# A two-layer graph network on one core: the products of the neighbour sums cut from 256 to 128 columns, each half with its own load of the counts

## The chip, the core and the metric

The kernel runs on one core of a Trainium2 chip. The core has five engines that run their own instruction streams and meet through semaphores: TensorE (PE, matrix products; its loads of the stationary operand are shown as PEld), VectorE (DVE), ScalarE (ACT), GpSimd (POOL) and SyncE (SP), and 16 DMA engines that they share. The metric is the device time of one execution in microseconds, lower is better.

## The reference, cut to what matters

A graph has 3125 nodes with 128 features and 100000 edges sorted by their target node. Two blocks are applied one after the other: a mean-aggregating network of two layers, then a network of two layers that aggregates in four ways. What matters here is what is summed or compared over each node's edges:

```python
# first block, twice
summed = segment_sum(x[src], dst)
mean   = summed / max(deg, 1)
out    = x @ W_self + mean @ W_neigh + b
# second block, twice (layers l = 0, 1)
h       = xi[dst] + xj[src] + b_pre
mean    = segment_sum(h, dst) / degc
mean_sq = segment_sum(h * h, dst) / degc
std     = sqrt(relu(mean_sq - mean * mean) + eps)
mx, mn  = segment_max(h, dst), segment_min(h, dst)
out = concat(x, agg, agg * amp, agg * att) @ W_post + b_post   # agg = mean, mx, mn, std
out = out @ W_lin + b_lin
```

A layer norm and a residual follow each layer.

## The kernel before

The nodes lie in 25 blocks (`NT`) of 125 (`NB`). In a first stage the kernel counts, for each pair of a target block and a source block, how many edges go from each source node to each target node; these counts are exact in bf16 and are stored to DRAM (`counts`, 25 blocks of 800 KB). A sum over the edges is then a matrix product: for a target block b, the sum over the 25 source blocks a of counts(a, b) transposed times the features of a. The features are split into three bf16 parts (`XS[.., a, c, ..]`, c = 0 to 2) whose sum is the fp32 value, so one target block takes 25 x 3 = 75 products. `add_block` (L1186 to L1195) issues them into one bank of PSUM, with the counts `A[.., slot, a, :]` as the stationary operand, loaded for each product, and 128 or 256 columns of `XS` as the moving one:

- first sums (inside the stage that makes the counts) and second sums (`second_sums`, L1520) have width 128 (`F`), 75 products for each of 25 blocks each;
- each of the two main scans (`main_scan`, one for each layer of the second block) has width 256: the values and their squares side by side, 75 products for each of 25 blocks.

**The main scan** also finds the maximum and minimum over the edges, in two ways. For each target node, up to one edge from each of 20 source blocks (`PICKED`) is picked by a product with a matrix of ones and zeros (`select`, L1295, product L1308; 6 products of 500 columns for two source blocks and four target blocks); the other edges, at most 432 in each of 128 lanes (`REST`), are gathered row by row and scanned. The work is laid out in 70 slots (`NSLOT`). In slot s the engines do:

- PE: the select of slot s+1, in some slots three products of weights (`use_operands`, L1279 to L1282) or two transposes (`turn_operands`, L1269), the pieces of the sums listed in `AHEAD[s]`, then the lift of slot s (`lift_absent`, L1313, product L1320, two products of 500 columns), and then the pieces in `BEHIND[s]`. A piece is one source block a of one target block b, three products (`piece`, L1335).
- DVE: `take_top` (L2233, or L2230 at the first pair of a group) takes the maximum with the selected values, waiting for the select; two rows of the scan (`scan_row`, L2281); `take_low` (L2251 or L2248) takes the minimum, waiting for the lift of this slot; then parts of the epilogue of one target block in some slots, and the slot's other rows of the scan.
- PE's select of slot s+2 waits for `take_low` of slot s, since both use the same two banks in turn; PE's lift of slot s waits for `take_top` of slot s.
- POOL: `gather_rest` (L1120) issues one indirect DMA for each of the 432 rows (L1132), into a ring of six batches of four rows. It waits until a batch's earlier rows are scanned and stored.
- ACT: negates each batch that has landed (L950), evacuates the sums of a block when its last piece is done (`take_sums`, L789), and loads the counts of the block after next (`load_block`, L824).
- SP: stores each batch of scanned rows (`rest_history`, L657, 512 KB) and loads the picks (L637, 640 KB).

The number of pieces in each slot comes from a table that is built before the kernel: a slot has (ahead, behind) = (0, 7) in 23 slots, (2, 11) in 19, (4, 9) in 7, (4, 10) and (2, 12) in 4 each, (0, 10) and (2, 2) in one each, and none in 11. So 35 slots of a scan have 27 to 36 products behind the lift, 23 have 21, and 12 have six or none.

The lines that the change touches:

```python
for a in range(a0, a1):
    for c in range(3):
        m = nc.tensor.matmul(acc[:, bank, 0:width], A[0:NB, slot, a, :], XS[0:NB, a, c, 0:width],
                             start=a == 0 and c == 0, stop=a == NT - 1 and c == 2)
```

Of the kernel before, what the change touches and what calls it, by code (L numbers as in the profile page):

```python
# [14 lines left out]
F = 128  # L15
N = 3125
E = 100000
NB = 125
NT = N // NB
# [196 lines left out]
def gnn_kernel(nc, x, src, dst, w_self1, w_neigh1, b1, w_self2, w_neigh2, b2,  # L216
# [3 lines left out]
    with ctx:  # L220
        def sb(name, shape, dt=F32):
            return ctx.enter_context(nc.sbuf_tensor(name, shape, dt))
# [28 lines left out]
        XS = big[:].bitcast(BF16).rearrange("p (a c f) -> p a c f", c=3, f=2 * F)  # L251
        EXT = big[:, 0:NT * 2 * F].rearrange("p (a f) -> p a f", f=2 * F)
        A = sb("A", [P, 2, NT, P], BF16)
# [157 lines left out]
        acc = ps[:, 0:5]  # L411
# [765 lines left out]
        def _(pe):  # L1177
# [8 lines left out]
            def add_block(k, b, bank, slot, width, a0, a1):  # L1186

                if a0 == 0:

                    pe.wait_ge(sums_out, b + (NT * k + 1))  # L1190
                for a in range(a0, a1):
                    for c in range(3):
                        m = nc.tensor.matmul(acc[:, bank, 0:width], A[0:NB, slot, a, :], XS[0:NB, a, c, 0:width],  # L1193
                                             start=a == 0 and c == 0, stop=a == NT - 1 and c == 2)
                if a1 == NT:  # L1195
                    m.then_inc(summed, 1)

# [12 lines left out]
            def make_block(b, slot, first=False):  # L1210

                for j in range(PIECES):
                    pe.wait_ge(onehots, b * (2 * PIECES) + (2 * j + 3))
                    pe.wait_ge(counted, b * PIECES + (j + 1))
                    h = (slot + j) % 2
                    for t in range(PT):
                        at = t // WT * CODES
                        m = nc.tensor.matmul(acc[:, h, at:at + CODES], hot_s[:, h, :, t],  # L1218
                                             hot_c[:, h, t],
                                             start=t % WT == 0, stop=t % WT == WT - 1)  # L1220
                    m.then_inc(tallied, 1)
                    if first and 0 < j < COLS:
                        turn_windows(j)
                    if not first and j > 1:
                        pe.wait_ge(counts_made, b * NG + (j - 1 - NG))
                        add_block(0, b - 1, 3 - slot, 1 - slot, F, (j - 2) * GT, (j - 1) * GT)
# [13 lines left out]
            with pe.Fori(0, NT // 2) as i:  # L1240
                make_block(i * 2 + 1, 1)
                make_block(i * 2 + 2, 0)
            pe.wait_ge(counts_made, NT * NG)
            add_block(0, NT - 1, 2, 0, F, 0, NT)
            pe.wait_ge(pe_go, 4)
            nc.tensor.matmul(acc[:, 3, 0:P], tiny[:, 4:5].to_broadcast([P, P]), ident[:],
                             start=True, stop=True)
            pe.wait_ge(upper_made, 2)
            nc.tensor.matmul(acc[:, 3, P:2 * P], run_count.to_broadcast([P, P]), upper,
                             start=True, stop=True).then_inc(small_mm, 1)  # L1250
# [74 lines left out]
            def main_scan(l):  # L1325
# [9 lines left out]
                def piece(b, a):  # L1335
                    if b == 0 and a % GT == 0:
                        pe.wait_ge(squares_ready, NG * l + a // GT + 1)
                    if a == 0:
                        pe.wait_ge(a_in[b % 2], 16 * (b // 2 + 1 + (k - 1) * ((NT + 1 - b % 2) // 2)))
                    add_block(k, b, b % 2, b % 2, 2 * F, a, a + 1)  # L1340
# [1131 lines left out]
```

## Time and profile before

| | us |
|---|---|
| median of 3 runs | 2370.49 (2369.53 to 2374.67) |
| the profiled execution | 2379.5 |
| its span | 2377.8 |
| first main scan, from the span's start | about 640 to 1385 |
| second main scan | about 1510 to 2252 |
| PE busy | 1499.0 |
| DVE busy | 1440.3 |
| POOL busy | 977.5 |
| ACT busy | 528.8 |

The span runs from the first to the last instruction in the profile. Busy time is the union of an engine's instructions. A row of a timeline gives the start, the duration, the engine, the line, the operation, and what was written and read, with the shapes; `xN` merges N equal ones, and in brackets stands how long the engine was idle before and what ended that. "issue" means that the profile shows nothing that the engine waited for; "remote" means that a semaphore was raised at a time at which no recorded instruction ended. A duration of one matmul is longer than the distance of two, since they are pipelined: paces are read from starts. PEclk is the granted clock of TensorE as a share of 2.4 GHz.

### The profile page before, as it was taken

To read this page: it belongs to the slowest core of one execution; us is meant where nothing else is said; L and a number is where in the kernel's file an instruction comes from. 1 tells how busy PE (TensorE), PEld (TensorE's weight loads), DVE (VectorE), ACT (ScalarE), POOL (GpSimd) and SP (SyncE) were. 2 spreads that over 40 slices of the span, in tenths; PEclk is the share of its full clock that TensorE was granted. 3 is DMA by queue.
4 is the path that set the end of the run, shared out by engine and by line. 5 is a ranking of instruction groups with operands and counts; after the bars stand their busy time and mean duration, and the time that the engine had idled before them with its cause. 6 is when DMAs were issued, how large, how long until landed. Compare 5 with 4: busy or idle time off the path is not lost.

```text
span 2377.8 us, 29952 instructions
## 1 busy us (share of the span) xinstructions
PE 1499.0 (63%) x10970; PEld 1032.1 (43%) x10970; DVE 1440.3 (61%) x2972; ACT 528.8 (22%) x1118; POOL 977.5 (41%) x1007
## 2 busy tenths in 40 slices
PE   0277777689547677677666537457675776767444
PEld 0167776679324344444344414224343443444222
DVE  7899997833466464555454437666454645555447
ACT  3377775101311111111111102311111111111101
POOL 4300000230356555555555540665565555545340
PEclk9798898989768787788777768777787878878677
DMA  4233333235235454555444431445454545544320
GB/s 113 77 132 128 124 125 126 91 128 189 94 116 199 139 175 169 169 171 172 158 163 139 133 113 47 159 153 169 156 197 141 183 156 169 169 158 160 112 87 25
DMA packets 131596, 332.07 MB, mean 140 GB/s; under 512 B 25040, under 2 KB 70176, under 8 KB 131086
## 3 DMA queue, kind: packets, MB, share of 16 engines
q1 hardware_dynamic: 74928, 159.93, 18.5%
q10 hardware_dynamic: 23470, 101.11, 12.2%
q0 software_dynamic: 33072, 69.45, 10.8%
q8 instruction: 67, 1.10, 0.2%
q14 instruction: 59, 0.48, 0.1%
HBM read 170.65 MB, written 159.77 MB: 139 GB/s over the span
## 4 chain that ended last, share of the span: by engine, by line
DVE 30%; PE 29%; another core or an unknown queue 17%; issue 15%; DMA 3%; POOL 3%; ACT 2%; ACTq 1%; DVEq 0%; POOLq 0%
PE ps L1193 15%; DVE scanned L2281 7%; PE ps L1308 4%; DVE accs L2251 4%; DVE scanned L1774 3%; DVE scanned L1771 3%; DVE scanned L1780 3%; DVE accs L2233 2%; PE ps L1320 2%; PE ps L1408 1%; PE ps L1218 1%; PE ps L1279 1%; PE ps L1281 1%; PE ps L1282 1%
## 5 line engine op out<-in xcount | busy, mean ns | idle before, releaser
L1132 POOL DMA_INDIRECT scanned<-table,rest_idx x864 | 846.8, 980 | 817.3 <-issue 237.6
L1193 PE MATMUL ps<-big,A 125*128 125x128 bf16 (+1 forms) x7500 | 808.7, 263 | 226.3 <-issue 215.3
L1193 PEld LDWEIGHTS ps<-big,A 125*128 125x128 bf16 x7500 | 627.7, 104 | 402.7 <-issue 305.7
L2251 DVE TENSOR_TENSOR accs<-accs,ps 128x1000 f32<-128x1000 f32 (+1 forms) x126 | 136.5, 1083 | 570.5 <-remote 488.8
L2281 DVE SCALAR_TENSOR_TENSOR scanned<-scanned,rest_neg 128x256 f32<-128x256 f32 x864 | 418.0, 484 | 51.0 <-issue 7.3
L1308 PE MATMUL ps<-S,big 126*128 126x500 bf16 (+1 forms) x840 | 244.0, 434 | 213.0 <-DVE accs L2251 123.5
L1308 PEld LDWEIGHTS ps<-S,big 126*128 126x128 bf16 x840 | 86.7, 112 | 327.9 <-DVE accs L2251 142.2
L950 ACT ACTIVATE scanned<-scanned 128x512 f32<-128x512 f32 x216 | 130.2, 621 | 306.5 <-DMA scanned<-table,rest_idx 276.3
L1218 PE MATMUL ps<-scanned 128*128 128x150 bf16 x1050 | 112.5, 247 | 72.3 <-DVE scanned L1780 64.7
L1151 POOL IOTA Y<- 128x784 int32 x1 | 0.8, 787 | 355.4 <-DVEq L2038 355.4
L1320 PE MATMUL ps<-S,lift 128*128 128x500 bf16 (+1 forms) x280 | 88.9, 397 | 78.9 <-DVE accs L2233 42.4
L2233 DVE TENSOR_TENSOR accs<-accs,ps 128x1000 f32<-128x1000 f32 (+1 forms) x126 | 135.8, 1078 | 0.5 <-DVE weights L2300 0.4
L814 ACT ACTIVATE A<-ps,tiny 128x450 bf16<-128x450 f32 x175 | 108.2, 635 | 84.7 <-PE ps L1218 40.6
L1408 PE MATMUL ps<-weights,scanned 128*128 128x384 f32 x200 | 90.6, 584 | 54.4 <-DVE scanned L2334 42.3
L1218 PEld LDWEIGHTS ps<-scanned 128*128 128x128 bf16 x1050 | 84.6, 131 | 90.0 <-ACT A L814 48.2
L789 ACT COPY sums_t<-ps 128x128 f32<-128x128 f32 x50 | 13.3, 267 | 479.2 <-remote 385.0
L1774 DVE TENSOR_TENSOR scanned<-scanned,H 128x900 bf16<-128x900 bf16 x175 | 108.8, 622 | 0.0
L1771 DVE TENSOR_TENSOR scanned<-scanned,H 128x750 bf16<-128x750 f16 x175 | 95.4, 545 | 8.6 <-PE ps L1218 8.2
L799 ACT ACTIVATE A<-A,tiny 128x640 bf16<-128x640 bf16 x125 | 99.5, 818 | 0.2 <-DVE S L1747 0.2
L1780 DVE TENSOR_TENSOR scanned<-scanned,H 128x768 bf16<-128x768 bf16 x175 | 96.6, 552 | 0.0
L923 ACT ACTIVATE operands_t<-operands_t 128x128 f32<-128x128 f32 x50 | 15.5, 309 | 311.1 <-DVE operands_t L1881 208.1
L1320 PEld LDWEIGHTS ps<-S,lift 128*128 128x128 bf16 x280 | 24.7, 106 | 120.2 <-DVE accs L2233 52.1
(394 smaller groups left out, 1430.7 us busy)
## 6 DMA issues: line engine op xcount, KB each, us to landing
rest_history<-scanned SPq DMA_DIRECT2D x216, 512.0 KB
A<-counts ACTq DMA_DIRECT2D x75, 800.0 KB
S<-picks SPq DMA_DIRECT2D x48, 640.0 KB
counts<-A ACTq DMA_DIRECT2D x25, 800.0 KB
picks<-S ACTq DMA_DIRECT2D x25, 640.0 KB
scanned<-table,rest_idx POOLq DMA_INDIRECT x864
table<-Y SPq DMA_DIRECT2D x10, 320.0 KB, 2.7
x_plus_h<-X SPq DMA_DIRECT2D x1, 1600.0 KB
```

The lines of the kernel that those rows point to most:

```text
L950: nc.scalar.activation(lanes[:, r, :, F:2 * F], lanes[:, r, :, 0:F], ACT.Copy, scale=-1.0)\
L1132: nc.gpsimd.indirect_dma_start(out=lanes[:, r, s, 0:F], out_offset=None, in_=tables[1 + l], in_offset=bass.IndirectOffsetOnAxis(ap=rest_id ...
L1193: m = nc.tensor.matmul(acc[:, bank, 0:width], A[0:NB, slot, a, :], XS[0:NB, a, c, 0:width], start=a == 0 and c == 0, stop=a == NT - 1 and ...
L1218: m = nc.tensor.matmul(acc[:, h, at:at + CODES], hot_s[:, h, :, t], hot_c[:, h, t], start=t % WT == 0, stop=t % WT == WT - 1)
L1308: m = nc.tensor.matmul(ps[:, bank + h, 0:len(blocks) * NB], XS[0:NB + 1, a, c, 0:F], pick[0:NB + 1, part % RING, 0:len(blocks), a % PART, ...
L1320: m = nc.tensor.matmul(ps[:, bank + h, 0:len(blocks) * NB], lift[:], pick[:, part % RING, 0:len(blocks), a % PART, 0:NB], start=False, sto ...
L1771: v.tensor_tensor(plain_s[:, h, 0:NB], iota_s[:, 0:NB], by_step(lows, n).unsqueeze(1).to_broadcast([P, NB, PT]), ALU.is_equal)\
L1774: v.tensor_tensor(hot_c[:, h].rearrange("p t (c u) -> p t c u", u=2), iota_c.rearrange("p (c u) -> p c u", u=2).unsqueeze(1) .to_broadcast ...
L1780: v.tensor_tensor(hot_s[:, h], plain_s[:, h], by_step(heavy, n).unsqueeze(1).to_broadcast([P, P, PT]), ALU.mult)\
L2233: v.tensor_tensor(top[:, :, 0:cols], top[:, :, 0:cols], ps[:, bank:bank + 2, 0:cols], ALU.max)\
L2251: v.tensor_tensor(low[:, :, 0:cols], low[:, :, 0:cols], ps[:, bank:bank + 2, 0:cols], ALU.min)\
L2281: v.scalar_tensor_tensor(this, last, rest_neg[:, i:i + 1], this, ALU.add, ALU.max)\
```

## The change

Each product of width 256 becomes two of 128 columns, one behind the other, with the same stationary operand, which is loaded for each. The first product of a target block (which starts the accumulation) and the last (which ends it) keep their width. Calls of width 128 issue what they did.

```diff
                 for a in range(a0, a1):
                     for c in range(3):
-                        m = nc.tensor.matmul(acc[:, bank, 0:width], A[0:NB, slot, a, :], XS[0:NB, a, c, 0:width],
-                                             start=a == 0 and c == 0, stop=a == NT - 1 and c == 2)
+                        first, final = a == 0 and c == 0, a == NT - 1 and c == 2
+                        step = width if first or final else F
+                        for f in range(0, width, step):
+                            m = nc.tensor.matmul(acc[:, bank, f:f + step], A[0:NB, slot, a, :],
+                                                 XS[0:NB, a, c, f:f + step], start=first, stop=final)
                 if a1 == NT:
                     m.then_inc(summed, 1)
```

PE's entries in two slots of a main scan, before (L1308 is the select, L1320 the lift, L1193 the sums, L1269 the transposes, L1279 to L1282 the products of weights):

```order
L1193 MATMUL ps<-big,A 128x256 x6
L1269 MATMUL ps<-ident,operands_t 128x128 x2
L1320 MATMUL ps<-S,lift 128x500 x2
L1193 MATMUL ps<-big,A 128x256 x36
L1308 MATMUL ps<-S,big 128x500 x6
L1279 MATMUL ps<-weights,C 128x384
L1281 MATMUL ps<-weights,operands_t 128x384
L1282 MATMUL ps<-weights,operands_t 128x384
L1320 MATMUL ps<-S,lift 128x500 x2
L1193 MATMUL ps<-big,A 128x256 x21
```

and the same two slots after the change, whose lines stand three further down (L1196 for L1193, L1311 for L1308, L1323 for L1320, and so on):

```order
L1196 MATMUL ps<-big,A 128x128 x12
L1272 MATMUL ps<-ident,operands_t 128x128 x2
L1323 MATMUL ps<-S,lift 128x500 x2
L1196 MATMUL ps<-big,A 128x128 x34
L1196 MATMUL ps<-big,A 128x256 x2
L1196 MATMUL ps<-big,A 128x128 x34
L1311 MATMUL ps<-S,big 128x500 x6
L1282 MATMUL ps<-weights,C 128x384
L1284 MATMUL ps<-weights,operands_t 128x384
L1285 MATMUL ps<-weights,operands_t 128x384
L1323 MATMUL ps<-S,lift 128x500 x2
L1196 MATMUL ps<-big,A 128x128 x42
```

Nothing changed its place: the 6, 36 and 21 products of 256 columns are 12, 70 (of which two are the last of a block and the first of the next, of 256 columns) and 42 in the same places. The other engines' instructions are the same.

## Rows read from the trace of the kernel before

**Rows 1.** The page: its first line, the busy times, the chain's lines, groups of L1193.

```profile
span 2377.8 us, 29952 instructions
...
PE 1499.0 (63%) x10970; PEld 1032.1 (43%) x10970; DVE 1440.3 (61%) x2972; ACT 528.8 (22%) x1118; POOL 977.5 (41%) x1007
...
PE ps L1193 15%; DVE scanned L2281 7%; PE ps L1308 4%; DVE accs L2251 4%; DVE scanned L1774 3%; DVE scanned L1771 3%; DVE scanned L1780 3%; DVE accs L2233 2%; PE ps L1320 2%; PE ps L1408 1%; PE ps L1218 1%; PE ps L1279 1%; PE ps L1281 1%; PE ps L1282 1%
...
L1193 PE MATMUL ps<-big,A 125*128 125x128 bf16 (+1 forms) x7500 | 808.7, 263 | 226.3 <-issue 215.3
L1193 PEld LDWEIGHTS ps<-big,A 125*128 125x128 bf16 x7500 | 627.7, 104 | 402.7 <-issue 305.7
```

**Rows 2.** Windows: busy us (x) by engine, granted clock, DMA share, GB/s.

```profile
640.00:1385.00 745.00, 483.43 (x2660) 294.27 (x2660) 404.86 (x735) 107.01 (x264) 409.27 (x421) 0.78 0.48 158
1510.00:2252.00 742.00, 481.86 (x2662) 293.25 (x2662) 408.45 (x739) 108.62 (x266) 413.29 (x423) 0.78 0.48 159
...
1044.50:1049.80 5.30, 5.30 (x19) 3.09 (x19) 4.93 (x8) 2.44 (x7) 0.00 (x0) 0.50 0.71 247
1058.30:1061.90 3.60, 3.60 (x34) 2.98 (x31) 1.20 (x2) 0.93 (x2) 2.70 (x3) 1.00 0.59 200
```

**Rows 3.** Waits of the whole span: who waited for whom, us, times, longest.

```profile
DVE accs L2251 <- remote: 488.8, 47, 19.6
...
POOL scanned L1132 <- DMA rest_history<-scanned: 233.3, 38, 12.2
...
POOL scanned L1132 <- DVE scanned L2281: 153.9, 53, 9.5
...
DVE accs L2248 <- remote: 50.6, 5, 17.0
```

**Rows 4.** Timeline of PE's products, 1032 to 1049 us (start, us, engine, line).

```profile
1032.33 1.44 PE L1308 MATMUL ps<-S,big 126*128 126x500 bf16 x6
...
1034.59 0.60 PE L1320 MATMUL ps<-S,lift 128*128 128x500 bf16 x2
1035.02 1.58 PE L1193 MATMUL ps<-big,A 125*128 125x256 bf16 x13
...
1038.14 0.28 PE L1193 MATMUL ps<-big,A 125*128 125x256 bf16 x1 [0.44 <-issue]
...
1044.49 2.72 PE L1193 MATMUL ps<-big,A 125*128 125x256 bf16 x12 [1.00 <-issue]
1047.01 2.70 PE L1308 MATMUL ps<-S,big 126*128 126x500 bf16 x6
```

**Rows 5.** Timeline of DVE, 1034 to 1053 us.

```profile
1044.62 1.20 DVE L2251 TENSOR_TENSOR accs<-accs,ps 128x1000 f32<-128x1000 f32 x1 [9.17 <-remote]
1045.73 3.15 DVE L2281 SCALAR_TENSOR_TENSOR scanned<-scanned,rest_neg 128x256 f32<-128x256 f32 x6
...
1052.25 1.20 DVE L2251 TENSOR_TENSOR accs<-accs,ps 128x1000 f32<-128x1000 f32 x1 [1.35 <-PE ps L1320]
```

**Rows 6.** Timeline of PE's loads in the same stretch.

```profile
1041.71 0.10 PEld L1193 LDWEIGHTS ps<-big,A 125*128 125x128 bf16 x1 [0.61 <-issue]
```

**Rows 7.** Timeline of POOL, 1026 to 1049 us: first and last of 12 gathers.

```profile
1027.42 0.95 POOL L1132 DMA_INDIRECT scanned<-table,rest_idx  x1 [4.73 <-DMA rest_history<-scanned]
...
1041.19 0.95 POOL L1132 DMA_INDIRECT scanned<-table,rest_idx  x1 [0.30 <-issue]
```

**Rows 8.** Timeline of PE in the second sums, 544 to 549 us.

```profile
544.25 4.36 PE L1193 MATMUL ps<-big,A 125*128 125x128 bf16 x75 [0.56 <-DMA A<-counts]
548.45 0.35 PE L1515 MATMUL ps<-small,scanned 128*128 128x25 f32 x2
```

**Rows 9.** Pieces of the chain that ended last: start, us, what.

```profile
122.38 1.60 PE ps L1193 x15
...
1058.31 3.60 PE ps L1193 x33
```

**Rows 10.** The page: DMA queues, packets, MB, share of 16 engines.

```profile
q8 instruction: 67, 1.10, 0.2%
```

## The prediction

> **What bounds the kernel now.** I read the page first, its span of 2377.8 us and the rows of L1193 [rows 1]; then the stretches by stage [rows 2]. The change touches only the products of 256 columns, and these stand in the two main scans: 745 and 742 us, 1487 of the span. In each the engines are little more than half busy: PE 483, DVE 405, POOL 409 us, at a mean granted clock of 0.78. So the scans are bound by hand-overs, and the waits say which [rows 3]: DVE stands 488.8 us in 47 waits ahead of L2251, put down to "remote", and L2248 adds 50.6 us in 5. L2251 waits for the "lift" product L1320, a product of PE. POOL waits 233.3 us for stores of scanned rows and 153.9 us for the scan itself.
>
> The most telling place is 1032 to 1052 us, engine by engine. PE starts the two lifts at 1034.59 and the products behind them [rows 4], yet DVE, which needs the second lift, starts L2251 at 1044.62, 9.17 us idle [rows 5]. In between, PE starts 13 products at full pace, then one or two entries, product or load, every 0.7 us (a product at 1038.14; a load at 1041.71, after 0.61 us of "issue") and is free again at 1044.49 [rows 4, 6]. Meanwhile POOL issues gathers every 1.25 us from 1027.42 to 1041.19 and then stops, with the ring full [rows 7]. I count what PE started between the end of the select of 1032.33 and the release: 31 products and 32 loads, some 62 entries. I read this so: **while POOL gathers without a pause, PE's completions reach nobody, and PE may run about 62 entries (loads and products counted alike) ahead of the oldest one not yet reported**. When POOL has been quiet for some 2.5 us, all is released. That limit counts entries, not columns, and the change doubles entries.
>
> **The change part by part.** It reaches 73 of 75 products in each of 25 blocks of two scans: 3650 products of 256 columns become 7300 of 128, so 3650 products and 3650 loads are added. The first and last of a block stay whole, and calls of width 128 (first and second sums) stay as they are. Nothing is moved between engines, no DMA or semaphore is added.
>
> (1) Array time. 33 products of 256 columns take 3.60 us, 109.1 ns each [rows 9], with the full clock granted (1.00, 2.4 GHz) [rows 2]. 75 of 128 columns, each with its own load, take 544.25 to 548.45, 4.20 us or 56.0 ns [rows 8], the pace of the same level. Two for one: 112.0 against 109.1, +2.9 ns. At the half clock (0.50) [rows 2] 12 of 256 columns take 1044.49 to 1047.01, 210 ns [rows 4], and 15 of 128 columns take 1.60 us in the first stage, 106.7 ns [rows 9]: 213 against 210, nothing or 3 ns. In all 3650 x 2.9 = 10.6 us of PE. L1193 holds 15% of the span in the chain of waits (357 us) and is busy 808.7 us [rows 1], so 0.44 of it lies on the path: **+5 us**, bounds 0 and 11.
>
> The loads: PEld's mean of 104 ns [rows 1] is longer than 56 ns, but in rows 8 each of the 75 products has its own load and keeps the 56 ns, so loads overlap there.
>
> Here a rule speaks against the change. The Trainium skill, page "TensorE: Matmul & The Clock Gate", section "Back-to-back issue gap", gives 81 ns per product as the sustained pace of load and product pairs of 128 columns; by it the change would add (162 - 109) ns x 3650 = 193 us of PE time, an estimate from that page. The 56.0 ns of rows 8 does not agree with it for this very form of product.
>
> (2) The run-ahead after a late release. There are 52 late releases (47 and 5) [rows 3]. Of a scan's 70 slots, 35 have 27 to 36 products behind the lift (33 is usual), 23 have 21, 12 have at most 6; I share the 52 out alike: 26, 17, 9.
> With 33 behind: in rows 4 the release found 12 of them not started. After the change the same 62 entries hold 12 half products ahead of the lift, 2 transposes and 2 lifts (32 entries) and then 15 half products; 51 of 66 are left. At the half clock that is 51 x 106.7 = 5.4 us against 2.5 us, +2.9; at the full clock 51 x 56.0 = 2.9 against 1.3, +1.6. The granted 0.78 [rows 2] is 44% half clock: +2.2 us.
> With 21 behind, after a select, 3 products of weights and the lift (16 entries), 23 of 42 half products fit, 19 are left: 1.1 us at full, 2.0 at half clock, where nothing was left before. The next select must wait for L2251 anyway, 1.20 us [rows 5], which covers the first case and leaves 0.8 of the second: +0.4 us.
> Sum: 26 x 2.2 + 17 x 0.4 = 64 us of PE lateness, 1.23 us for a release.
>
> How much of it is passed on? After the release of 1044.62 DVE comes to the next L2251 at 1052.25, having waited 1.35 us for PE's lift [rows 5]: PE is the later of the two there, so the lateness reaches DVE. But POOL's next gathers wait only for rows scanned right behind L2251, which no PE work delays; so the stretch from release to the next blockade stays as long, and less fits into it. From release to release is 1487 / 52 = 28.6 us, 10.4 of it blocked, 18.2 open. 1.23 us off 18.2 is 6.8% less per round, 7.3% more rounds. What a round costs beyond gathering is POOL's pause: 233.3 + 153.9 = 387 us in all [rows 3]; 7.3% of that is **+28 us**. Bounds: nothing, if leftovers hide behind DVE's rows; 64 us, if all is passed on. I take the 28, since DVE's 1.35 us says the lateness is passed on and POOL's rows say it doesn't add up linearly.
>
> (3) Code. 7300 entries are added to some 21,940 of PE (10970 products and as many loads [rows 1]), a third; the instruction queue moved 67 packets in 0.2% of 16 engines' span [rows 10], 76 us or 1.1 us each. The second sums run at the new density [rows 8] without a gap in 75 products, so I cost the fetch at zero, covered by fetching ahead; with that cover gone, a third of 67 packets at 1.1 us is 25 us.
>
> Sum: 5 + 28 = +33 us, less what a shift of phase may give either way, rounded to +30. The profiled execution took 2379.5 us with a span of 2377.8, 9 us above the median 2370.49 of the runs; the sum gives 2409.5 for it, and **2400 us** for the median.
>
> **Rivals.**
> - No change (chance 0.18, 2370 to 2377). The leftovers end before DVE needs the next lift: 3.15 us of scan rows lie between [rows 5]. For: the select after the leftovers must wait for L2251 in any case. Against: the 1.35 us. Then only the 5 us of (1) are left. I count 0.14 of it as within 0.2%, which is about what a measurement here tells from no change (4.7 us), and 0.04 as slower.
> - Passed on in full (0.14). The lateness of 64 us adds up, and short delays become blockades, since sooner or later every lift has twice the entries ahead of it: 64 + 5 = +69, 2440; up to 2470.
> - Loads bound (0.04). If a load cannot overlap its neighbours beside the gathers, a pair takes 104 ns [rows 1]: 208 for 109, +99 ns x 3650 = 361 us of PE, 0.44 on the path, +159 us, 2530. Rows 8 speak against it. The rule of the Trainium skill named above is a milder form of it.
> - Faster, by the clock (0.12). PE now stands still after 62 entries less often with all its columns done; more columns are left for after the release, so a longer unbroken run follows it and the full clock may come sooner. The price is in the select: six products take 1.44 us at the full clock (1032.33) and 2.70 at the half (1047.01) [rows 4], 1.26 us apart. 44% of 140 selects, 62, run at the half clock; if half of them turn full, 39 us, of which I take half as on the path: -20, 2350. It decides if the mean granted clock of the scans rises from 0.78 to above 0.85.
> That the change doesn't do what it says is excluded by the order of PE's entries.
>
> **How the numbers follow.** Forecast (2380 to 2430) 0.52, no change 0.18, in full 0.14, loads 0.04, clock 0.12. The range 2366 to 2442 leaves out most of the clock's case and the parts above 2442, under 2 in 10. Faster 0.12, same 0.14, slower 0.74 (0.52 + 0.04 + 0.14 + 0.04). The forecast's own range is 2380 to 2430.
>
> **What would show it.** Right: DVE's waits ahead of L2251 by "remote" stay near 10 us each but grow in number from 47 to about 50 or more; after a release PE has some 50 half products ahead of its select instead of 12 whole ones; POOL's pauses for stores and scans grow from 387 to some 415 us; pairs of 128 columns in the scans stand 56 ns apart at the full clock; the first 640 us are unchanged. Wrong: a pace above 60 ns there (loads), "issue" gaps between products without gathers beside them (code), a granted clock above 0.85 (clock), or as many entries after the lift as before, in columns (the limit does not count entries).

## The result, and the profile after

The change takes **2540.09 us** (median of 4 runs, 2522.75 to 2546.5) against 2370.01 us before (4 runs, 2360.3 to 2374.67): ratio **1.071, 95% interval 1.065 to 1.078**. That is +170 us; +30 was forecast, and the range ended at 2442. The profiled execution took 2522.75 us, 143 us of span more than that of before. One execution of the kernel before in set 4 below took 4572 us, and no ratio uses it.

The page of the changed kernel: first line, busy times, the instruction queue, the chain by engine and by line, the groups of the sums' products and loads.

```profile
span 2521.0 us, 37252 instructions
...
PE 1585.1 (63%) x14620; PEld 1154.9 (46%) x14620; DVE 1440.4 (57%) x2972; ACT 527.6 (21%) x1118; POOL 976.1 (39%) x1007
...
q8 instruction: 95, 1.56, 0.2%
...
PE 43%; issue 24%; DVE 21%; another core or an unknown queue 4%; DMA 2%; POOL 2%; ACT 2%; ACTq 1%; DVEq 0%; POOLq 0%
PE ps L1196 24%; PE ps L1311 6%; DVE scanned L2284 4%; DVE scanned L1777 3%; PE ps L1323 3%; DVE scanned L1774 2%; DVE scanned L1783 2%; DVE accs L2254 2%; PE ps L1282 2%; DVE accs L2236 2%; PE ps L1284 2%; PE ps L1285 1%; PE ps L1411 1%; PE ps L1221 1%
...
L1196 PE MATMUL ps<-big,A 125*128 125x128 bf16 x11150 | 884.5, 236 | 427.1 <-issue 417.5
L1196 PEld LDWEIGHTS ps<-big,A 125*128 125x128 bf16 x11150 | 752.1, 106 | 570.9 <-issue 525.4
```

Against [rows 1], DVE works exactly as long and POOL nearly so, PE 86 us longer (76 of it in the sums' products), and the idle time ahead of the sums' products that is put down to "issue" has nearly doubled, from 215.3 to 417.5 us; in the chain these products hold 24% instead of 15%.

The windows of the changed kernel, in the columns of [rows 2], over the first stage and over a stretch with each scan in it:

```profile
0.00:640.00 640.00, 415.98 (x5248) 380.30 (x5249) 486.93 (x972) 275.90 (x503) 90.95 (x100) 0.87 0.34 120
640.00:1440.00 800.00, 508.43 (x4410) 341.31 (x4409) 385.38 (x686) 102.38 (x253) 403.37 (x414) 0.76 0.44 143
1600.00:2400.00 800.00, 522.78 (x4481) 352.14 (x4480) 403.62 (x732) 105.78 (x262) 404.62 (x418) 0.76 0.45 147
```

The scans now fill these 800 us and do less of DVE's and POOL's work in them than before in 745 and 742. All the time is lost there, and the waits of the whole span say in what form (who waited for whom, us, times, longest):

```profile
PEld ps L1196 <- issue: 525.4, 602, 11.5
PE ps L1196 <- issue: 417.5, 545, 11.3
DVE accs L2254 <- PE ps L1323: 384.5, 58, 24.3
...
POOL scanned L1132 <- DMA rest_history<-scanned: 344.0, 47, 17.7
DVE accs L2254 <- remote: 278.0, 32, 15.5
...
POOL scanned L1132 <- DVE scanned L2284: 196.7, 53, 16.5
...
DVE accs L2251 <- PE ps L1323: 59.2, 4, 23.5
...
DVE accs L2251 <- remote: 22.7, 2, 11.6
...
DVE accs L2254 <- issue: 20.1, 5, 10.4
```

and in the kernel before, beside [rows 3], the three that were not shown:

```profile
DVE accs L2251 <- PE ps L1320: 79.9, 37, 14.2
...
DVE accs L2251 <- issue: 1.1, 4, 0.5
DVE accs L2248 <- PE ps L1320: 1.1, 4, 0.4
```

DVE's waits for the lift come to 764 us in 101 waits (384.5 + 278.0 + 59.2 + 22.7 + 20.1) instead of 622 in 97 (488.8 + 50.6 + 79.9 + 1.1 + 1.1). The difference is as large as that of the spans, 143 us. And their nature turned: the part by "remote" fell from 539 us in 52 to 301 in 34, while the part put down to the lift rose from 81 us in 41 to 444 in 62. The names are rough, since they go by the records of raised semaphores, and some of these are missing. The recorded end of each lift divides the same waits without them: before, 158 us lie ahead of the lift's end and 463 behind it; after, 537 ahead and 227 behind (495 and 282, 501 and 279 in the two later traces of the change). So what grew is the time in which the lift has not run yet. POOL's pauses for stores and for the scan grew from 387 to 541 us.

Below, a *hold* is a stretch in which PE's completions are held up, and the *release* is its end. One such place in the changed kernel, 997 to 1010 us. POOL:

```profile
998.74 0.94 POOL L1132 DMA_INDIRECT scanned<-table,rest_idx  x1 [0.30 <-issue]
999.99 0.95 POOL L1132 DMA_INDIRECT scanned<-table,rest_idx  x1 [0.30 <-issue]
```

PE and DVE in the same timeline:

```profile
998.91 0.26 PE L1196 MATMUL ps<-big,A 125*128 125x128 bf16 x1 [1.15 <-issue]
...
999.63 0.39 PE L1196 MATMUL ps<-big,A 125*128 125x128 bf16 x2 [0.46 <-issue]
...
1001.76 0.27 PE L1196 MATMUL ps<-big,A 125*128 125x128 bf16 x1 [1.73 <-issue]
...
1002.49 1.01 PE L1311 MATMUL ps<-S,big 126*128 126x500 bf16 x2 [0.47 <-issue]
...
1003.91 1.83 PE L1311 MATMUL ps<-S,big 126*128 126x500 bf16 x4 [0.41 <-issue]
...
1005.53 1.48 PE L1282 MATMUL ps<-weights,C 128*128 128x384 f32 x2
...
1006.81 1.48 PE L1284 MATMUL ps<-weights,operands_t 128*128 128x384 f32 x2
...
1008.09 1.17 PE L1285 MATMUL ps<-weights,operands_t 128*128 128x384 f32 x2
...
1009.10 0.59 PE L1323 MATMUL ps<-S,lift 128*128 128x500 bf16 x2
...
1009.73 1.20 DVE L2254 TENSOR_TENSOR accs<-accs,ps 128x1000 f32<-128x1000 f32 x1 [19.02 <-PE ps L1323]
```

POOL's last gather ends at 1000.94. PE is freed at 1003.91, 3 us later (2.5 us in the kernel before: [rows 7] end at 1042.14, and DVE starts at 1044.62 [rows 5]). But in [rows 4] PE had passed the lift long before the release; here half products kept it at one entry each 0.7 us so long that at the release it still has four products of the select, six of weights (two records for each of the three) and the lift ahead of it, 5.2 us. DVE has stood for 19 us.

Over the whole trace of the kernel before, 54 lifts reached DVE more than 1 us late. For 38 of them POOL's last gather had ended 1.0 to 4.3 us earlier (median 2.8); the other 16, one eighth of the late time, were passed on while POOL went on gathering. So a completion in a hold comes late rather than never, and a stop of POOL is the usual release, not the only one. The limit holds throughout: in the traces of the kernel before and of the change no more than 63 of PE's entries start between a lift and the DVE instruction that waits for it. And the step of 0.7 us is the mark of a hold: PE's starts lie 0.68 to 0.75 us apart 339 times in the kernel before and 479 times in the changed one, but 18 times in the unsplit run without gathers (set 1), with a single late lift, and 9 times in the run with a third of the split (set 2), with none.

### The profile page after: what moved, and what is told of

Read it like the earlier page. It is cut to its first block, busy times and chain, and to the rows that moved or that the text cites. A ratio compares the mean times of both kernels' runs of the same rounds, so it can differ in the third digit from the quotient of the medians.

```text
span 2521.0 us, 37252 instructions
## 1 busy us (share of the span) xinstructions
PE 1585.1 (63%) x14620; PEld 1154.9 (46%) x14620; DVE 1440.4 (57%) x2972; ACT 527.6 (21%) x1118; POOL 976.1 (39%) x1007
## 4 chain that ended last, share of the span: by engine, by line
PE 43%; issue 24%; DVE 21%; another core or an unknown queue 4%; DMA 2%; POOL 2%; ACT 2%; ACTq 1%; DVEq 0%; POOLq 0%
PE ps L1196 24%; PE ps L1311 6%; DVE scanned L2284 4%; DVE scanned L1777 3%; PE ps L1323 3%; DVE scanned L1774 2%; DVE scanned L1783 2%; DVE accs L2254 2%; PE ps L1282 2%; DVE accs L2236 2%; PE ps L1284 2%; PE ps L1285 1%; PE ps L1411 1%; PE ps L1221 1%
## 5 line engine op out<-in xcount | busy, mean ns | idle before, releaser
L1196 PE MATMUL ps<-big,A 125*128 125x128 bf16 x11150 | 884.5, 236 | 427.1 <-issue 417.5
L1196 PEld LDWEIGHTS ps<-big,A 125*128 125x128 bf16 x11150 | 752.1, 106 | 570.9 <-issue 525.4
L2254 DVE TENSOR_TENSOR accs<-accs,ps 128x1000 f32<-128x1000 f32 (+1 forms) x126 | 136.5, 1083 | 682.6 <-PE ps L1323 384.5
L1311 PE MATMUL ps<-S,big 126*128 126x500 bf16 (+1 forms) x840 | 248.1, 432 | 102.0 <-issue 57.1
L1311 PEld LDWEIGHTS ps<-S,big 126*128 126x128 bf16 x840 | 83.9, 113 | 216.5 <-issue 137.3
L1323 PE MATMUL ps<-S,lift 128*128 128x500 bf16 (+1 forms) x280 | 88.0, 397 | 69.6 <-DVE accs L2236 50.5
L1411 PEld LDWEIGHTS ps<-weights,scanned 128*128 128x128 f32 x200 | 40.8, 226 | 76.9 <-DVE scanned L2337 39.5
```

What stands on the lines that cost most here:

```text
L1196: m = nc.tensor.matmul(acc[:, bank, f:f + step], A[0:NB, slot, a, :], XS[0:NB, a, c, f:f + step], start=first, stop=final)
L1311: m = nc.tensor.matmul(ps[:, bank + h, 0:len(blocks) * NB], XS[0:NB + 1, a, c, 0:F], pick[0:NB + 1, part % RING, 0:len(blocks), a % PART, ...
L1323: m = nc.tensor.matmul(ps[:, bank + h, 0:len(blocks) * NB], lift[:], pick[:, part % RING, 0:len(blocks), a % PART, 0:NB], start=False, sto ...
L1411: m = nc.tensor.matmul(acc[:, b % GT, 0:3 * F], lhs_ext[:, SLOT[b % GT], h * P:(h + 1) * P], weights[:, w + 4 + 3 * h:w + 7 + 3 * h, :] .r ...
L2254: v.tensor_tensor(low[:, :, 0:cols], low[:, :, 0:cols], ps[:, bank:bank + 2, 0:cols], ALU.min)\
```

## The experiments

Five sets of runs were made, each on a chip of its own, beside runs of the kernel before on the same chip. Ratios are to those runs.

**Set 1: what in the change costs, and whether it needs the gathers** (before: 2345.95 us, 7 runs).

The added loads alone (3650 entries instead of 7300, not one product or column more):

```diff
+                        if width > F and 0 < 3 * a + c < 3 * NT - 1:
+                            nc.tensor.ldweights(A[0:NB, slot, a, :])
                         m = nc.tensor.matmul(acc[:, bank, 0:width], A[0:NB, slot, a, :], XS[0:NB, a, c, 0:width],
```

> The kernel before, with one more load of the same counts ahead of each of the 3650 middle products of the main scans: 3650 entries more for PE, no product and no column more. If each entry costs the same during the blockades (theory A, entries), this is half of the change's 7300 entries: half of its +170 us, 2430 to 2480. If it is the loads that bound a pair (theory B), the count of loads is that of the change and the cost is near all of it, 2520 to 2550. If only products count (their completions, or the half columns), 2365 to 2380.

Measured: 2431.92 us, ratio 1.036 (1.030 to 1.042): +86 us for half of the entries, half of the change's +170. Loads that write what already stands in the array cost as much for each entry as loads and products together: 23.6 ns here, 23.3 in the change. **Entries cost, not columns.**

Both kernels with POOL gathering only the first 24 rows of 864; ACT's wait for a batch becomes one for a count that POOL raises, so the scan works on old rows and the output is not the reference's. The same edit on both:

```diff
-                act.wait_ge(main.landed[r], 16 * BATCH * ring_uses(r, n + 1))
+                act.wait_ge(main.landed[r], 16 * BATCH)
+                act.wait_ge(zeroed, n + 2)
...
-                    for s in range(BATCH):
+                    pool.sem_inc(zeroed, 1)
+                    for s in range(BATCH if n < LANES_RING else 0):
```

> The kernel before without the row gathers of the main scans, except the first 24 of 864: POOL passes the batches on by a semaphore alone. Theory A: the blockades vanish, so DVE's long waits by 'remote' (539 us in 52) go and the time falls by 300 us or more, below 2100. If the blockades come from the stores and loads of SP and ACT, or from PE itself, they stay, and the time falls by less than 150 us.

> The changed kernel without the same gathers. Theory A: with no gathers there is no limit on entries, and the split costs only array time: at most 15 us above e3_no_gather_before. Theory B (loads, or the pace of pairs) and theory C (fetching code for a third more entries): the split costs 100 us or more (B) or 25 us or more (C) above e3_no_gather_before, since loads and code are the same.

Measured: 1795.46 us (0.764, 0.758 to 0.769) and 1798.13 us (0.765, 0.761 to 0.770). Without gathers the 7300 entries cost 3 us, less than the runs of either kernel differ among themselves (11 to 17 us), and not 170. The windows of 640 to 1090 us, first of the unsplit kernel, then of the split one:

```profile
640.00:1090.00 450.00, 387.08 (x2654) 273.84 (x2654) 396.75 (x722) 105.66 (x264) 12.08 (x13) 0.95 0.57 200
```

```profile
640.00:1090.00 450.00, 392.88 (x4477) 300.67 (x4475) 396.73 (x724) 104.45 (x262) 9.06 (x9) 0.94 0.57 200
```

A scan that takes 745 us in [rows 2] is done in some 450, by either kernel. The split adds 5.8 us of PE there, 1823 more products, and DVE covers it. Of DVE's waits for the lift, one (9.3 us) is still put down to "remote" in the first and none in the second, instead of 52. PE is busy for 86% of these 450 us, so a cost near 170 us could not hide there. That rules out the array's pace, the loads and the fetching of code as the main cost, and ties it to POOL's gathers.

The kernel before, with POOL at most three batches ahead of the scan instead of five:

```diff
-                    if n >= LANES_RING - 1:
-                        pool.wait_ge(main.scan_ops, BATCH * (n - LANES_RING + 1) + 1)
+                    if n >= 3:
+                        pool.wait_ge(main.scan_ops, BATCH * (n - 3) + 1)
```

> The kernel before, with POOL kept to three batches (12 rows) ahead of the scan instead of five to six. Theory A: a blockade lasts until POOL runs out of room, so each gets shorter, 5 us instead of 10, though there may be more of them: 2250 to 2370, with DVE's 'remote' waits well under 539 us. Rival: the depth is needed to cover the latency of gathers and stores, and POOL's own waits grow: 2400 or more.

Measured: 2301.8 us, ratio 0.977 (0.970 to 0.983). POOL waits more for the scan (338.7 us instead of 153.9), and the kernel gains 44 us by it: DVE's waits by "remote" fall from 488.8 us in 47 to 338.9 in 39, and the part of all its waits behind the lift's end from 463 us to 240.

**Set 2: the dose, and the split with a slower POOL** (before: **1936.87 us**, 19 runs). A third of the split (`step = F` only for c = 1); fewer entries, by one product of 512 columns for c = 0 and 1:

```diff
+                    if width > F:
+                        nc.tensor.matmul(acc[:, bank, 0:2 * width], A[0:NB, slot, a, :],
+                                         XS[0:NB, a, 0:2].rearrange("p c f -> p (c f)"), start=a == 0, stop=a == NT - 1)
+                        m = nc.tensor.matmul(acc[:, bank, 0:width], A[0:NB, slot, a, :], XS[0:NB, a, 2, 0:width],
+                                             start=False, stop=a == NT - 1, skip_group_check=True)
+                        continue
```

and each of the split and the merged form with POOL three batches ahead. In the merged forms the upper half of the bank is not added to the lower, so their output is not the reference's.

> Only the middle one of the three products per source block (c = 1) is done as two of 128 columns; the other two stay whole. 1250 products and 1250 loads are added, 2500 entries, against 7300 of the change and 3650 of the run with loads alone. Theory A (each entry that stands in front of a lift while PE's completions are held up costs its 0.70 us step in some of the rounds, on the whole linear: 170 us / 7300 = 23 ns an entry): +58 us, ratio 1.02 to 1.03. Rival D (a threshold: the small addition still fits in the 62 entries and the cost begins later): under +20 us, ratio below 1.01. Rival S (it saturates: the first added entries cost the most): over +90 us, ratio above 1.038.

> The other direction: in the main scans the products c = 0 and c = 1 of a source block, which share their counts, are one product of 512 columns into the whole bank, and c = 2 one of 256 columns. Two products and two loads instead of three and three, with the same columns; 2500 entries fewer than before. The addition of the bank's upper half to the lower is left out, so the output is not the reference's. Theory A: the cost per entry holds on this side too, -58 us, ratio 0.97 to 0.98. Rival C (columns or array time decide, not entries): no change, ratio 0.995 to 1.005. Rival D (threshold at the number of entries of before): under -20 us.

> The change, with POOL kept at most three batches ahead of the scan (as in the run that was 2.3% faster than before). Against that run (2301.8 us, ratio 0.977) it adds the 7300 entries of the change. Theory A: bursts of gathers are shorter (12 instead of up to 20 and more), so a blockade ends earlier, but lifts still stand behind their entries: +100 to +170 us, 2400 to 2470 us, ratio 1.02 to 1.05; DVE's waits put down to PE are again most of it. Rival B (an added load or product costs its 23 ns whatever POOL does, beside any gathers): +170 us or more, ratio 1.05 and above. Rival E (bursts of 12 gathers are short enough for the 62 entries): below +40 us, ratio under 0.995.

> POOL kept at most three batches ahead, and the products c = 0 and c = 1 as one of 512 columns (the addition of the bank's upper half is left out, so the output is not the reference's). 2500 entries fewer than the run of three batches ahead alone (2301.8 us, ratio 0.977). Theory A: the two gains lie on the same waits but add up in most: another -30 to -58 us, 2245 to 2270 us, ratio 0.955 to 0.967. Rival: with short bursts the entries no longer matter, ratio 0.975 to 0.98.

Measured: 1937.39 us (0.999, 0.998 to 1.001), 1933.67 (0.999, 0.997 to 1.000), 2043.95 (1.054, 1.050 to 1.058) and 2036.07 (1.051, 1.048 to 1.054). As a dose these say nothing, for here the same kernel before takes 409 to 433 us less than on the other chips, and entries cost next to nothing: 9800 of them lie between the last two runs, and 8 us. The slower POOL, 2.3% of gain in set 1, loses 5% with either form (it was not run here by itself).

What differs stands in the waits of the run with a third split:

```profile
ACT scanned L950 <- DMA scanned<-table,rest_idx: 857.7, 211, 9.1
...
POOL scanned L1132 <- issue: 228.6, 750, 0.3
DVE accs L2254 <- PE ps L1323: 207.0, 81, 8.8
```

and in its timeline of DVE:

```profile
1003.72 1.20 DVE L2254 TENSOR_TENSOR accs<-accs,ps 128x1000 f32<-128x1000 f32 x1 [3.13 <-PE ps L1323]
...
1009.91 1.19 DVE L2254 TENSOR_TENSOR accs<-accs,ps 128x1000 f32<-128x1000 f32 x1
...
1019.02 1.20 DVE L2254 TENSOR_TENSOR accs<-accs,ps 128x1000 f32<-128x1000 f32 x1 [2.67 <-PE ps L1323]
```

There is no wait by "remote", though POOL gathers every 1.25 us without a pause through this whole stretch. In none of the traces of sets 2 and 4 does a lift reach DVE more than 1 us late. **On this chip PE's completions are not held up while POOL gathers.** POOL then never waits for the scan for more than 0.3 us and sets the pace itself: 432 gathers of 1.25 us are 540 us a scan.

Is it a faster chip in all? The first 640 us and the first gather of the scan, in the kernel before (which ran on a chip of the other kind), and then in the run with a third split:

```profile
0.00:640.00 640.00, 412.97 (x5251) 374.95 (x5251) 488.42 (x974) 276.23 (x503) 91.69 (x101) 0.89 0.35 121
...
624.12 1.10 POOL L1132 DMA_INDIRECT scanned<-table,rest_idx  x1 [121.88 <-DMA table<-Y]
```

```profile
0.00:640.00 640.00, 414.81 (x5288) 378.52 (x5289) 501.21 (x993) 280.88 (x512) 106.07 (x116) 0.89 0.36 125
...
604.00 1.09 POOL L1132 DMA_INDIRECT scanned<-table,rest_idx  x1 [103.48 <-DMA table<-Y]
```

A little: the first gather comes 20 us, 3%, sooner. But the granted clock is the same there, DVE is busy for 1439.2 us of the whole span here and for 1440.3 there, and of the 439 us between the two spans 382 lie in the two scans, which take 556 and 557 us from the first lift to the last instruction that waits for one, instead of 750 and 745.

**Set 3: the change and the merged form again** (before: 2369.09 us, 7 runs).

> The change itself, once more, because the kernel before took 1937 us in the last set of runs and 2346 to 2370 us in the others. Two theories on what makes that difference. Theory H (held-up completions come with the chip the runs fall on): where the kernel before takes about 1937 us, no wait of DVE is put down to remote, POOL gathers without a pause and sets the end, and the change costs nothing, ratio 0.995 to 1.01; where it takes about 2350 us, the waits by remote are there and the ratio is 1.06 to 1.08 again. Rival K (the split costs its array time and loads anyway, and 1937 us is a chip that is faster in all): ratio 1.03 or more even at 1937 us.

> The products c = 0 and c = 1 as one of 512 columns, 2500 entries fewer, again (the addition of the bank's upper half is left out, so the output is not the reference's). On a chip where the kernel before takes about 2350 us: theory A says 23 ns an entry on this side too, -58 us, ratio 0.97 to 0.98; rival D (threshold) less than 20 us of gain, ratio above 0.99. On a chip where it takes 1937 us: 0.999 as before, by theory H.

Measured: the change 2536.95 us, ratio 1.070 (1.063 to 1.077), with 353.3 us of DVE's waits by "remote": a chip with held-up completions, and theory H's second case. The merged form 2335.72 us, ratio 0.986 (0.980 to 0.991): -33 us for 2500 entries fewer, 13 ns each, between theory A's 58 and the threshold's 20. So the curve is bent: an entry less is worth little more than half of what an entry more costs. The waits say why: before, only 158 of DVE's 622 us lie ahead of the lift's end, where fewer entries can help; the merged form brings these down to 74, while the part behind the lift's end grows from 463 to 502. (Its products of 512 columns are another difference, and no run separates the two.)

**Sets 4 and 5: does a pause of POOL release PE?** One edit, on the kernel before and on the change:

```diff
                             .then_inc(main.landed[r], 16)
+                    if n % 2 == 1:
+                        pool.wait_ge(main.landed[r], 16 * BATCH * ring_uses(r, n + 1))
```

Set 4 (before: 1940.1 us, 13 runs) fell on a chip without held-up completions:

> The kernel before, with one edit on POOL: behind every eighth gather POOL waits until its last four gathers have landed, some 3 us in which it issues none. Where completions are held up (before about 2350 us), theory A (a pause of POOL releases PE's completions): bursts of 8 gathers, 10 us, and a pause of about 3 us, 13 us for 8 rows, 700 us for the 432 of a scan; DVE's waits by remote become shorter (mean below 7 us instead of 10.4) and the scans go from 745 us to 680 to 720, 2240 to 2320 us in all, ratio 0.95 to 0.98. Rival R (a release needs a longer pause, or another cause): waits by remote stay near 10 us each and the pauses come on top, above 2400 us. Where completions are not held up (before about 1937 us) the pauses only cost: 108 of 3 us, +250 to +330 us.

> The change, with the same pause of POOL behind every eighth gather. Where completions are held up, theory A: in a hold of at most 12 to 13 us PE comes past its 62 entries later than in one of 20 us, fewer slow steps stand ahead of a lift, and the split costs less than its 170 us: +40 to +120 us over the run with the pause alone, below 2430 us, ratio to before 0.97 to 1.03. Rival (the cost of an entry does not depend on the length of a burst): +170 us over the run with the pause alone. Where completions are not held up: within 10 us of the run with the pause alone.

> Only the product c = 1 of three is split, 2500 entries added, again. Where completions are held up: theory A (linear, 23 ns an entry) +58 us, ratio 1.02 to 1.03; by the 34 us that 2500 fewer gave, a bent line would put it at +35 to +50 us; threshold under +20 us, ratio below 1.01. Where they are not held up: ratio 0.999 again.

> The change with POOL at most three batches ahead of the scan, again. Where completions are held up: against the same without the split (2301.8 us, ratio 0.977), theory A +100 to +170 us, ratio to before 1.02 to 1.05; rival B (each entry has its price whatever POOL does) +170 us or more, ratio 1.05 and above; rival E (bursts of 12 gathers are short enough) below +40 us, ratio under 0.995. Where they are not held up: ratio 1.054 again.

Measured: 2181.07 us (1.125, 1.121 to 1.129), 2181.97 (1.125, 1.121 to 1.129), 1936.68 (0.999, 0.997 to 1.000), 2037.94 (1.052, 1.047 to 1.056). The pauses cost 241 us, a little under the 250 to 330 expected; the whole split costs 1 us on top. The third of the split fell on a chip without held-up completions both times, so where completions are held up the cost of added entries rests on two doses, 3650 and 7300. Set 5 (before: 2367.83 us, 7 runs) fell on a chip with held-up completions:

> The change itself. Where the kernel before takes about 1937 us: theory H, ratio 0.995 to 1.005, since POOL's gathers set the end of the scans there; rival K, 1.01 or more. Where it takes about 2350 us: 1.06 to 1.08 as before.

> The kernel before with POOL's pause of some 3 us behind every eighth gather. Where completions are not held up: 1.125 again. Where they are: theory A 2240 to 2320 us, ratio 0.95 to 0.98, waits by remote with a mean below 7 us; rival R (a release needs a longer pause or another cause) above 2400 us, waits by remote near 10 us.

> The change with the same pause. Where completions are not held up: within 10 us of the run with the pause alone. Where they are: theory A +40 to +120 us over the run with the pause alone, ratio to before 0.97 to 1.03; rival (an entry's cost does not depend on the length of a burst) +170 us over it.

Measured: the change 2535.7 us (1.069, 1.063 to 1.075); **the pause alone 2246.24 us (0.947, 0.940 to 0.954)**; the split with the pause 2328.98 us (0.983, 0.977 to 0.988). Theory A's times and waits came true, its ratio for the pause by 0.003 more than that (0.947 where 0.95 to 0.98 stood). The waits of the kernel with the pause:

```profile
DVE accs L2253 <- PE ps L1322: 237.8, 57, 9.5
POOL scanned L1132 <- DMA scanned<-table,rest_idx: 233.3, 91, 6.4
...
DVE accs L2253 <- issue: 97.4, 18, 8.1
DVE accs L2253 <- remote: 86.9, 26, 7.4
...
DVE accs L2250 <- PE ps L1322: 26.8, 6, 6.5
...
DVE accs L2250 <- issue: 11.5, 4, 6.6
...
DVE accs L2250 <- remote: 10.3, 2, 5.5
```

POOL stands 233.3 us in its new pauses, 2.6 us each, and DVE's waits for the lift come to 471 us instead of 622; those of L2253 by "remote" have a mean of 3.3 us instead of 10.4. Of all these waits 99 us lie behind the lift's end instead of 463. One pause in its timeline, POOL and then DVE:

```profile
912.36 0.94 POOL L1132 DMA_INDIRECT scanned<-table,rest_idx  x1 [0.30 <-issue]
916.66 0.95 POOL L1132 DMA_INDIRECT scanned<-table,rest_idx  x1 [3.36 <-DMA scanned<-table,rest_idx]
```

```profile
916.29 1.20 DVE L2253 TENSOR_TENSOR accs<-accs,ps 128x1000 f32<-128x1000 f32 x1 [8.96 <-PE ps L1322]
```

DVE gets its lift inside the pause, 3.0 us after the last gather's end. In this kernel the split costs 83 us (2328.98 - 2246.24), half of the 168 to 170 that it costs without pauses: an entry's price depends on how POOL's gathers are grouped, and the rival of that run, a price that does not, falls. So the kernel with the pause beats both kernels where completions are held up, even with the split, and neither where they are not (set 4). None that I ran is faster on both kinds.

## Why the prediction was wrong in size

- *What bounds the kernel now*: right in the main. Held-up completions, a run-ahead that counts loads and products alike (63 at most, with loads alone too), a release some 3 us after POOL's last gather: loads alone cost half (set 1), no gathers no cost (set 1), a pause releases (set 5). "Reach nobody" was too strong: 16 of 54 late lifts were passed on while POOL gathered.
- *(1) array time, +5 us, bounds 0 and 11*: right as far as the runs can tell; 3 us without gathers, and 5.8 us more of PE's busy time in a scan, 11.6 for both where 10.6 was forecast. The half products of the changed scans start 56.0 ns apart at the full clock and 107 ns at the half (medians), so the pace of [rows 8] was the one to use, and "loads bound" falls with its milder form. That rival's 2530 us lies near the result, for another reason.
- *(3) code, 0*: right. The instruction queue moved 95 packets instead of 67 [rows 10], and with no gathers beside it no more than the 3 us was lost.
- *(2) the run-ahead, 64 us of PE lateness, of which +28 on the path*: **this step failed, in its size.** It priced only half products left over *behind* a lift after a release, at 56 or 107 ns each. It took for granted that PE reaches the lift within a hold, as in [rows 4], because the 62 entries sufficed for it there. With twice the entries ahead of them the next select and lift often come too late for that, so the entries at 0.7 us each, and behind the release the select and the products of weights, stand ahead of the lift: the waits ahead of the lift's end grew by 379 us (158 to 537), those behind it shrank by 236 (463 to 227), and DVE's waits as a whole grew by 143 where +28 was forecast. The rival "passed on in full" named this ("sooner or later every lift has twice the entries ahead of it") and was right in kind; but it, too, was costed with the 64 us of the leftovers and ended at 2470.
- *The damping, 28 of 64*: not borne out. The argument was that POOL's next burst hangs on nothing that PE delays. Its pauses for stores and scans grew by 154 us (387 to 541), not by 28. What I had passed over is in [rows 5]: the rows of the scan that POOL waits for stand behind L2251 on DVE's queue, and L2251 waits for the lift.
- *What would show it*: the waits by "remote" were to stay near 10 us and grow in number from 47. Their mean on L2254 is 8.7 us, and they became fewer, 32. The clock of the scans fell from 0.78 to 0.76, so the rival "faster, by the clock" has its sign wrong.

The change was never run alone on a chip where completions are not held up. The runs there with a third of it, and with all of it behind POOL's pauses, say that it would cost about nothing; that is an inference. Why the chips of sets 2 and 4 differ from the others is open: the traces show that they do, not by what. No chip of the five sets was used twice, so it is not shown either that it is the chip and not the moment of the runs; within each of these sets the runs of the kernel before that the ratios use agree within 1.2%.

Open too is what holds the completions up. Where it happens the trace has fewer records of raised semaphores, of DVE, ACT and the DMAs as well: for the 864 rows of the scan 572 in the kernel before and 605 in the changed one, but 856 without gathers (set 1) and 860 with the third split (set 2). DVE's completions reached the lift all the same: in the kernel before it stood more than 1 us behind the `take_top` that it waits for only 8 times of 140, and 2.0 us at most. Every execution here was recorded by the profiler, so no run shows whether completions would be held up without the recording; that rival is untested.

## What to carry to other kernels

When an engine's completions reach nobody for a while, the price of an instruction is not its duration but its place in the queue ahead of the next product that somebody waits for: count entries up to that product, in the kernel as it will be and not as it is, and price those beyond the run-ahead at the slow step (a sum that was not tried here). A producer that runs far ahead can be the cause of the wait that it later suffers; a short pause is then cheaper than its absence, but here it took 5% off on one kind of chip and added 12% on the other, so such an edit is to be timed on more than one chip.

## What the runs showed of the hardware

- The same kernel has medians of 2346 to 2370 us in four sets of runs and 1937 and 1940 in two, on other chips, 18% apart, with a first stage 3% apart. In the four, PE's completions come late while POOL issues indirect DMAs every 1.25 us, up to 18 us after the lift's end in the kernel before, and most of the late ones 1.0 to 4.3 us after it stops; in the two they come in time while it gathers without a pause.
- Held up, PE runs at most 63 entries ahead of the lift, loads and products alike, and then starts one or two per 0.70 us. In this kernel that makes an added entry worth 23 ns (+86 us for 3650, +170 for 7300), a removed one 13 ns (-33 us for 2500), an added one 11 ns with POOL's pauses (83 us for 7300), and nothing that the runs can tell without gathers (3 us for 7300).
- Without gathers the whole kernel takes 1795 us even on a chip of the first kind: 24% of its time there is this one interaction together with the waits for the gathered rows.
